# Attention scores, sums and weighted values on small float32 tiles of the array, in a cross-attention and expert block

## The reference

```
x   = x + xattn(layernorm(x), ctx)          # x (4, 512, 512), ctx (4, 64, 512)
x   = x + ffn(layernorm(x))

xattn: q = h Wq^T + bq, k = ctx Wk^T + bk, v = ctx Wv^T + bv      # 16 heads of 32
       p = softmax(where(attend, clip(q k^T / sqrt(32), +-50), -50))
       layernorm(rs * ((p v) Wo^T + bo)) * gamma + beta
ffn:   8 experts of width 16, the two with the largest router weights:
       sum_e gate_e * silu(h down_e^T) up_e^T
```

## Time and profile before

| | us |
|---|---|
| median of 2 runs | 241.1 (240.43 to 241.77) |
| profiled execution, its own time | 242.23 |
| its span | 240.5 |
| PE busy | 213.7 (89%) |
| DVE busy | 174.7 (73%) |
| ACT busy | 111.5 (46%) |
| POOL busy | 93.6 (39%) |

### The profile page before, as it was taken

The page is one execution under the profiler, slowest core; times in us unless marked ns, Lnnn a source line. Parts: engine busy times, 40 slices in busy tenths (PEclk is TensorE's granted clock), DMA queues, the critical chain, the costliest instruction groups (busy, mean ns, idle before and its releaser), DMA issues.

```text
span 240.5 us, 3478 instructions
## 1 busy us (share of the span) xinstructions
PE 213.7 (89%) x1184; PEld 170.8 (71%) x1184; DVE 174.7 (73%) x414; ACT 111.5 (46%) x196; POOL 93.6 (39%) x160
## 2 busy tenths in 40 slices
PE   0399999899999999999699999999999999997744
PEld 0288675488887778898486788987867898775622
DVE  2766295585769778839977888478968768989783
ACT  2454675366023579641345586525263732314720
POOL 5842002089964145201585326022673101326520
PEclk9999999999999999999999999999999999997985
DMA  7999300405000000000022000000211000001124
GB/s 221 286 393 307 149 3 0 145 33 177 0 0 0 3 0 0 4 0 0 0 90 87 0 3 0 0 4 0 87 47 41 3 0 3 0 1 44 44 104 157
DMA packets 9316, 14.65 MB, mean 61 GB/s; under 512 B 1618, under 2 KB 2642, under 8 KB 9300
## 3 DMA queue, kind: packets, MB, share of 16 engines
q1 hardware_dynamic: 8704, 14.44, 17.0%
q10 hardware_dynamic: 596, 0.01, 0.1%
HBM read 10.25 MB, written 4.19 MB: 60 GB/s over the span
## 4 chain that ended last, share of the span: by engine, by line
PE 70%; DVE 12%; ACT 7%; DMA 4%; issue 4%; POOL 1%; SPq 1%; DVEq 0%; ACTq 0%
PE ps_r L336 43%; PE ps_v L415 8%; PE ps_t L360 7%; PE ps_v L446 5%; PE ps_r L403 5%; DMA wk<-wk_t 4%; ACT wk L633 2%; DVE d_st L940 1%; ACT stage L650 1%; PE ps_v L449 1%; DVE ln_st L851 1%; DVE hs L946 1%; DVE stage L905 1%; ACT kbd L681 1%; ACT q_hi L638 1%
## 5 line engine op out<-in xcount | busy, mean ns | idle before, releaser
L415 PE MATMUL ps_v<-vbd,stage 128*128 128x66 f32 x256 | 31.5, 273 | 0.7 <-DVE stage L905 0.4
L415 PEld LDWEIGHTS ps_v<-vbd,stage 128*128 128x128 f32 x256 | 30.4, 192 | 1.7 <-issue 1.3
L614 ACT CAST attt_hi<-ps_t 128x512 fp32r<-128x512 f32 x32 | 17.8, 588 | 24.1 <-PE ps_t L360 23.7
L336 PE MATMUL ps_r<-hst_hi,wq_hi 128*128 128x512 f32 x64 | 26.3, 410 | 0.0
L638 ACT ACTIVATE q_hi<-ps_r,bq_sb 128x512 fp32r<-128x512 f32 x16 | 11.0, 689 | 31.3 <-PE ps_r L336 31.3
L336 PE MATMUL ps_r<-hst_hi,wq_lo 128*128 128x512 f32 x64 | 25.3, 395 | 0.0
L336 PE MATMUL ps_r<-wo_lo,attt_hi 128*128 128x512 f32 x64 | 25.3, 395 | 0.0
L336 PE MATMUL ps_r<-wo_hi,attt_hi 128*128 128x512 f32 x64 | 25.2, 394 | 0.0
L336 PE MATMUL ps_r<-wo_hi,attt_lo 128*128 128x512 f32 x64 | 25.2, 394 | 0.0
L336 PE MATMUL ps_r<-hst_lo,wq_hi 128*128 128x512 f32 x64 | 25.2, 394 | 0.0
L861 DVE TENSOR_TENSOR attt_lo<-ps_t,attt_hi 128x512 fp32r<-128x512 f32 x32 | 21.2, 684 | 3.9 <-ACT attt_hi L614 3.7
(11 more groups left out here) (115 smaller groups left out, 471.3 us busy)
## 6 DMA issues: line engine op xcount, KB each, us to landing
out<-xs SPq DMA_DIRECT2D x16, 256.0 KB, 2.0
xs<-x SPq DMA_DIRECT2D x3, 1024.0 KB, 5.5
xs<-x SPq DMA_DIRECT2D x2, 512.0 KB, 4.4
wk<-wk_t SPq DMA_DIRECT2D x1, 1024.0 KB, 9.7
stage<-wq_t SPq DMA_DIRECT2D x1, 1024.0 KB, 11.8
xs<-wv_t SPq DMA_DIRECT2D x1, 1024.0 KB, 13.9
xs<-wo_t SPq DMA_DIRECT2D x1, 1024.0 KB, 15.9
stage<-ctx_t SPq DMA_DIRECT2D x1, 512.0 KB, 6.1
```

The costliest lines, as they stand in the source:

```text
L336: last = pe.matmul(dst, w, m, start=start and i == 0, stop=stop and i == n - 1)
L415: mmi = pe.matmul(ps_v[k][:, i * VW:(i + 1) * VW], probs[:, p, t * P:(t + 1) * P], vbd[:, b, p, :], start=True, stop=True)
L614: act.copy(dst, ps_t[ring_t.bank(part, use)][:, 0:c * P].rearrange("p (c n) -> p c n", c=c)).then_inc(done, 1)
```

## The change

Scores: `scores(b, r)` now does half of the heads at a time, 8 plain float32 matmuls of 32 array rows by 64 columns, each with one head's keys as the stationary operand and its 512 query columns streamed; four row groups and two column halves make eight tiles. Query and key are no longer split, so `q_lo`, `k_hl` and `kbd` go, and ACT alone empties the query banks. Sums: `sums(b, g)` multiplies the exponentials by a matrix of ones and zeros, 16 matmuls of 128 rows by 32 columns with 128 streamed columns, four accumulated in each of four column groups; the reciprocals come out with 128 elements in a partition, and `spread` copies them by 16 `stream_shuffle` of 128 columns to all channels of a head. Weighted values: `weigh(b, g)` holds 64 by 32 values as the stationary operand and streams the 512 exponentials of a head, 8 matmuls to a group. The result is channels by tokens, so `att_transpose` goes, and `att` is split chunk by chunk; `project` waits for all four chunks. `x1t` gets a buffer of its own, `att` moves from `wk` to `hs`. All orders are written anew, with a first step of its own.

```diff
-R_STEP = ["S0", "S1", "S2", "S3", "q2", "q3", "S4", "S5", "S6", "S7", "Q0", "W0", "W1", "Q1", "U0", "U1", "U2", "U3",
-          "W2", "W3"]
-R_FIRST = ["S0", "S1", "S2", "S3", "q2", "q3", "V0", "V1", "S4", "S5", "S6", "S7", "Q0", "W0", "W1", "Q1", "W2", "W3"]
+R_STEP = ["S0", "S1", "S2", "S3", "q2", "q3", "S4", "S5", "S6", "S7", "Q0", "Q1", "W0", "W1", "U0", "U1", "U2", "U3", "W2", "W3"]
+R_FIRST = ["S0", "S1", "S2", "S3", "q2", "q3", "S4", "S5", "S6", "S7", "V0", "V1", "Q0", "Q1", "W0", "W1", "W2", "W3"]
...
-T_STEP = ["n0", "n1", "h0", "h1", "h2", "h3", "n2", "n3", "c0", "c1", "a0", "c2", "c3", "a1"]
-T_LAST = ["n0", "n1", "n2", "n3", "c0", "c1", "a0", "c2", "c3", "a1", "n0+", "n1+", "n2+", "n3+", "a0+", "a1+"]
-V_LAST = ["f0", "v00", "f1", "v01", "v10", "v11", "v20", "f2", "f3", "v21", "v30", "v31", "f0+", "f1+", "f2+", "f3+"]
-V_STEP = ["f0", "f1", "v00", "v01", "v10", "v11", "v20", "v21", "f2", "f3", "v30", "v31"]
+T_FIRST = ["h0", "h1", "h2", "h3"]
+T_STEP = ["n0", "n1", "h0", "h1", "h2", "h3", "n2", "n3", "a0", "a1"]
+T_LAST = ["n0", "n1", "n2", "n3", "a0", "a1", "n0+", "n1+", "n2+", "n3+", "a0+", "a1+"]
+V_LAST = ["f0", "f1", "s0", "f2", "s1", "f3", "v0", "v1", "v2", "v3", "f0+", "f1+", "f2+", "f3+"]
+V_FIRST = ["s0", "s1", "v0", "v1", "v2", "v3"]
+V_STEP = ["f0", "f1", "s0", "s1", "v0", "v1", "v2", "v3", "f2", "f3"]
...
         hs = sb("hs", [P, KC, H])
-        cen = hs
...
-        kbd = sb("kbd", [P, 2 * KC, 2 * T], F32R)
...
-        vbd = sb("vbd", [P, B, NP, VW])
+        k_sb = sb("k_sb", [P, KC, B * T])
+        v_sb = sb("v_sb", [P, B, 2, P])
+        sum_ones = sb("sum_ones", [P, NT, 4, 2 * NT])
         up_out = sb("up_out", [P, NT, H])
-        q_hi, q_lo = split("q", [P, KC, S])
+        q_sb = sb("q_sb", [P, KC, S])
...
         attt_hi, attt_lo = split("attt", [P, NT, KC, P])
-        x1t_hi, x1t_lo = attt_hi, attt_lo
+        x1t_hi, x1t_lo = split("x1t", [P, NT, KC, P])
...
-            def scores(b, c):
-                uses = [f"S{2 * c + i}" for i in range(2)]
-                out = [ps_r[take(b, use)] for use in uses]
-                for which, (k_part, q_part) in enumerate(((c, q_hi), (c, q_lo), (KC + c, q_hi))):
-                    for i in range(2):
-                        r = slice(2 * HD * i, 2 * HD * (i + 1))
-                        mmi = pe.matmul(out[i][:, :], kbd[r, k_part, :], q_part[r, c, :],
-                                        start=which == 0, stop=which == 2)
-                        if which == 2:
+            def scores(b, r):
+                wanted = [(b - 1, "Q0"), (b - 1, "Q1")] if r == 0 else [(b, "q2"), (b, "q3")]
+                pe.wait_ge(q_ok, max(ring_r.count(part, use) for part, use in wanted))
+                out = [ps_r[take(b, f"S{4 * r + i}")] for i in range(4)]
+                for j in range(2):
+                    c = 2 * r + j
+                    for i in range(4):
+                        rows_in = slice(HD * i, HD * (i + 1))
+                        mmi = pe.matmul(out[i][j * T:(j + 1) * T, :], k_sb[rows_in, c, b * T:(b + 1) * T],
+                                        q_sb[rows_in, c, :], start=True, stop=True)
+                        if j == 1 and i % 2 == 1:
                             mmi.then_inc(s_full, 1)
-            def weigh(b, t, g):
-                k = take_one(ring_v, b, f"v{t}{g}", v_free)
-                if t == 0:
-                    pe.wait_ge(probs_ok, KC * b + 2 * g + 2)
+            def sums(b, g):
+                k = take_one(ring_v, b, f"s{g}", v_free)
+                pe.wait_ge(probs_ok, KC * b + 2 * g + 2)
+                for n in range(NT):
+                    for i in range(4):
+                        mmi = pe.matmul(ps_v[k][HD * i:HD * (i + 1), 0:P],
+                                        sum_ones[:, n, :, :].rearrange("p a m -> p (a m)"),
+                                        probs[:, 4 * g + i, n * P:(n + 1) * P], start=n == 0, stop=n == NT - 1)
+                mmi.then_inc(v_full, 1)
+            def weigh(b, g):
+                bank = [ps_v[take_one(ring_v, b, f"v{2 * g + j}", v_free)] for j in range(2)]
                 for i in range(4):
-                    p = 4 * g + i
-                    mmi = pe.matmul(ps_v[k][:, i * VW:(i + 1) * VW], probs[:, p, t * P:(t + 1) * P],
-                                    vbd[:, b, p, :], start=True, stop=True)
-                mmi.then_inc(v_full, 1)
-            def att_transpose(b, t):
-                pe.wait_ge(v_free, ring_v.count(b, f"v{t}1"))
-                transposes(b, f"c{t}", chunks(att, t))
+                    for j in range(2):
+                        rows_in = slice(T * j, T * (j + 1))
+                        mmi = pe.matmul(bank[j][HD * i:HD * (i + 1), :], v_sb[rows_in, b, g, HD * i:HD * (i + 1)],
+                                        probs[rows_in, 4 * g + i, :], start=True, stop=True)
+                        if i == 3:
+                            mmi.then_inc(v_full, 1)
             def project(b, t):
...
-                pe.wait_ge(t_free, ring_t.count(b, f"c{t}"))
+                pe.wait_ge(attt_lo_ok, KC * (b + 1))
                 k = take(b, f"W{t}")
                 pairs = [(ones_k[:, :], bo_hl[:, :])]
...
+            def step(b):
+                x1n_transpose(b, b - 1, 0)
+                scores(b, 0)
+                query(b, 2)
+                x1n_transpose(b, b - 1, 1)
+                query(b, 3)
+                down(b, (0,))
+                down(b, (1,))
+                scores(b, 1)
+                hs_transpose(b, b + 1, 0)
+                hs_transpose(b, b + 1, 1)
+                hs_transpose(b, b + 1, 2)
+                sums(b, 0)
+                hs_transpose(b, b + 1, 3)
+                x1n_transpose(b, b - 1, 2)
+                x1n_transpose(b, b - 1, 3)
+                query(b, 0)
+                sums(b, 1)
+                query(b, 1)
+                weigh(b, 0)
+                weigh(b, 1)
+                down(b, (2,))
+                down(b, (3,))
+                hid_transpose(b, b - 1, 0)
+                project(b, 0)
+                project(b, 1)
+                up(b, 0)
+                hid_transpose(b, b - 1, 1)
+                up(b, 1)
+                up(b, 2)
+                up(b, 3)
+                project(b, 2)
+                project(b, 3)
...
+            def att_hi(b, c):
+                act.wait_ge(v_free, ring_v.count(b, f"v{c}"))
+                act.copy(attt_hi[:, :, c, :], att[:, c, :].rearrange("p (t n) -> p t n", t=NT)).then_inc(attt_hi_ok, 1)
...
+            def att_lo(b, c):
+                dve.wait_ge(attt_hi_ok, KC * b + c + 1)
+                dve.tensor_tensor(attt_lo[:, :, c, :], att[:, c, :].rearrange("p (t n) -> p t n", t=NT),
+                                  attt_hi[:, :, c, :].bitcast(F32), ALU.subtract).then_inc(attt_lo_ok, 1)
...
-            def normalise(b, halves):
-                def values_of(half):
-                    return ps_v[ring_v.bank(b, f"v{half}")][:, 0:4 * VW].rearrange("p (n w) -> p n w", n=4)
-                def reciprocals(half):
-                    t, g = int(half[0]), int(half[1])
-                    dve.wait_ge(v_full, ring_v.count(b, f"v{half}"))
-                    dve.reciprocal(rz[:, t, g, :, :], values_of(half)[:, :, 2 * HD:VW]).then_inc(rz_ok, 1)
-                def product(half):
-                    t, g = int(half[0]), int(half[1])
-                    order = [u[1:] for u in V_STEP if u[0] == "v"]
-                    dve.wait_ge(rz_ok, 2 * NT * b + order.index(half) + 1)
-                    dve.tensor_tensor(att[:, t, 4 * 2 * HD * g:4 * 2 * HD * (g + 1)].rearrange(
-                                          "p (n s d) -> p n s d", n=4, s=2),
-                                      values_of(half)[:, :, 0:2 * HD].rearrange("p n (s d) -> p n s d", s=2),
-                                      rz[:, t, g, :, :].unsqueeze(3).broadcast_to([P, 4, 2, HD]), ALU.mult
-                                      ).then_inc(v_free, 1)
-                reciprocals(halves[0])
-                for half, following in zip(halves, halves[1:]):
-                    reciprocals(following)
-                    product(half)
-                product(halves[-1])
+            def reciprocals(b, g):
+                dve.wait_ge(v_full, ring_v.count(b, f"s{g}"))
+                dve.reciprocal(rz[:, g, :], ps_v[ring_v.bank(b, f"s{g}")][:, 0:P]).then_inc(v_free, 1)
+            def spread(b, g):
+                dve.wait_ge(v_free, ring_v.count(b, f"s{g}"))
+                if b < B - 1:
+                    dve.wait_ge(t_full, ring_t.count(b, f"h{2 * g + 1}"))
+                for j in range(2):
+                    for n in range(NT):
+                        dve.stream_shuffle(att[:, 2 * g + j, n * P:(n + 1) * P], rz[:, g, :], [NT * j + n] * 32
+                                           ).then_inc(spread_ok, 1)
+            def product(b, c):
+                dve.wait_ge(spread_ok, 2 * NT * (2 * b + c // 2) + NT * (c % 2 + 1))
```

(47 more changed lines are left out.)

562 lines of the change are left out of this document (247 added, 315 removed).

## The result

The changed kernel takes 269.5 us (267.57 and 271.50) against 241.1 before: ratio 1.118, 95% interval 1.081 to 1.155. It is slower. The profiled execution is one of 267.57 us with a span of 265.8 (before 240.5). The time of 269.5 lies inside the range, 229 to 277, and "slower" had the largest of the three chances. But the number, 243, is 26 us too low, and the rival that stood for "slower" is not what happened: that the time lies in the range is luck, since the forecast case itself ended at 252 and the upper part of the range came from that rival.

What follows compares the result with a forecast made beforehand. PE was taken to bound the middle of the kernel. First element -3.0 us, elements 1 and 2 together -0.8, last +5.5: +1.7 on 241.1 gives 242.8, rounded to 243; range for 8 in 10, 229 to 277.

Steps and rivals of the forecast that it cites:

- the forecast case: Whole kernel: tiles run side by side but PE is held up by waits; 234 to 252 us, chance 0.40.
- The price of the tiles: PE's score, sum and value groups: all tiles of a group run at once, 1.1 us per group.
- The sum of -22.4 us: PE's matmul and transpose work over all four elements: 6.6 us replaces 12.2, so -5.6 per element.
- The slower rival: Small-tile groups: a float32 matmul's second record holds up the next tile in program order; 283 us, or 265; chance 0.30.
- scores behind the centring: An element's first scores need banks freed by centring the previous element's W3; +1.4 us, 1.9 in the last element.
- second weighing: In elements 1 and 2 it needs both banks of the first, so waits for two products and two hops; +1.6 us.
- down 2: In elements 1 and 2 it needs the bank of product 2, which stands behind att_lo 0 and 1; +1.1 us.
- Elements 1 and 2, transposes: Six groups share two banks; each third waits for a `_lo` subtraction behind clips on DVE: +0.2 and about +1.3 us.
- project 0's 0.6: In elements 1 and 2 it needs all four att_lo, the last behind a cross addition waiting for down 2; +0.6 us.
- The old wait of 2.2: PE's wait for DVE in the middle of the kernel before; expected to go, -2.2 us in each of elements 1 and 2.
- 3.1 us of old waits: First element: 1.1 for the value blocks and 2.0 from last scores to first weighing were to go, -3.1 us.
- the faster rival: Whole kernel: the new waits overlap instead of adding, half of about 30 us gone; 230 us, chance 0.27.

Runs made afterwards that it cites:

- e1_warm: Changed kernel plus 93 filler matmuls on constant operands placed where PE waited; 257.2 us, ratio 1.065.
- e4_split: Changed kernel with each score and value matmul cut into two of 256 columns, one behind the other on the same tile; 270.0 us, ratio 1.118.
- e10_beta: Changed kernel with POOL's beta additions of the first two elements moved away from the first element's att_lo, and value_blocks(1) moved; 269.2 us, ratio 1.114.
- e5_warm_less: Changed kernel with e1_warm's fillers, copies in place of the reciprocals and one shuffle per chunk instead of four; 257.4 us, ratio 1.065.
- e9_halves: Changed kernel with weighted values cut by tokens instead of heads, and some calls moved to suit; 260.1 us, ratio 1.075.
- e12_both_warm: e11_both plus 84 filler matmuls in ten places; 256.7 us, ratio 1.057.
- e8_scores_only: Kernel before with only its scores changed, to four small-tile float32 matmuls per chunk; 241.9 us, ratio 0.9985.
- e11_both: Changed kernel with the edits of e9_halves and e10_beta together; 258.3 us, ratio 1.064.
- e6_reorder: Changed kernel with the same instructions in another order, both queries ahead of the scores in elements 1 to 3; 285.5 us, ratio 1.176.

## Why the prediction was right or wrong

**The price of the tiles: right.** 1.1 us was forecast per group, 1.02 to 1.13 measured, 1.08 for the sums. The sum of -22.4 us can be read too: the end of PE's last matmul less its idle time is 237.35 - 14.65 = 222.7 us before; with the clock held (e1_warm), fillers left out, it is 252.38 - 51.63 = 200.8, a difference of 21.9, with 8 and 10 us of half clock in the two up to there.

**The slower rival: its mechanism is refuted** (e4_split), though the time lies in its 265 to 283. The Trainium skill ("TensorE: Matmul & The Clock Gate", Part 3) has matmuls in strict program order of start and end. The groups of the changed kernel fit this, with eight first records and then eight second ones. The first group of e4_split does not: eight records start 13 to 18 ns apart, and three more rounds of eight begin 0.24, 0.45 and 0.67 us behind the first. The records do not name their tile, but with eight to a round a tile's second matmul starts behind the first ones of tiles that come later in the program. Here the measurement decides, and neither the second record nor a second matmul of one tile holds back the next tile, which was my reading.

**The waits: most of the named ones were right, their sum was 11 us too small.** Single waits, forecast and measured: scores behind the centring 1.4 in elements 1 and 2 and 1.9 in the last, measured 1.8, 1.6 and 2.0; query 2 behind the exponential 1.2 and 1.2; second weighing 1.6 and 1.6; down 2 1.1 and 0.9. By windows, which put the wait for the centring in the element before, idle time was to rise by 4.0, 5.2, 5.7 and 9.2 us and rose by 10.3, 6.7, 9.1 and 9.4. What failed:
- Elements 1 and 2, transposes: 1.5 us was forecast for each element; 3.0 and 3.5 were measured, of which the first, 1.9 each time, was entered as 0.2, as if it replaced a wait of the first weighing; the trace of before has only 0.2 us of waiting by weighings in each of these elements.
- Elements 1 and 2, up 0: its wait for the copy of a query, 1.1 in each, was not in the sum. Against it, project 0's 0.6 did not come.
- The old wait of 2.2 was taken off twice, as if element 2 had one like it. Rows 1 shows 50.80 less 49.53, 1.3 us of idle time in all there.
- In the first element 3.1 us of old waits were taken off, but PE had been idle for 1.3 in it: the 2.0 between the last scores and the piece at 49.09 in the chain was PE's own transposes and the beginning of the weighing:
```profile
46.70 0.43 PE L403 MATMUL ps_r<-q_hi,kbd 64*128 64x512 f32 x2
47.06 1.09 PE L360 MATMUL ps_t<-ident,hs 128*128 128x128 f32 x8
47.99 2.21 PE L415 MATMUL ps_v<-vbd,stage 128*128 128x66 f32 x16
```
- Project 0 of the first element waited 5.3, not 3.6, which e10_beta puts down to POOL running beside att_lo. And the wait of query 0 there, 1.4, behind hs_lo, with value_blocks(1) ahead of it on VectorE, was not in the sum.
- In the last element the sum came out, but in part by luck. Up to the second weighing 4.2 us was forecast and 4.7 measured, of which 3.2 are for a gating that the prediction had put behind it, since hidden transposes stand between the two weighings; up to project 0 5.7 was forecast and 3.2 measured. Small waits that were not in the forecast fill the difference.

**The clock: named, not priced.** The last sentence of the prediction set it aside. It is nearly half of what is missing, 12 us by e1_warm. The half clock rose from 11 us, all in the tail, to 44, and the longer stretches come in or behind waits: at 64.9 (in the wait of 5.3), 116.1, 170.8, and from 215.1 through the three waits of the last element. The profile had a row for it: in the tail of before, where PE is busy for 14.89 of 25.00 us, the clock is 0.78. A forecast that adds 24 us of waits to elements which had 6 should have charged some of that, though no row could say how much: the wait of 2.2 us in element 1 of before left the clock at 1.00.

**The sum again.** From before to after, -22 of work, +36 of idle time (51.0 less 14.7) and +11 of half clock (after's 262.7 - 51.0 = 211.7, less e1_warm's 200.8) make +25, which is the difference of the two spans, 265.8 less 240.5. The forecast was -22.4 and +24.1. (In the faster rival, half of about 30 us is 15, and 13 was taken off; its chance of 0.27 did not hang on that.)

**The sizes of VectorE's operations: one wrong, harmless.** Reciprocal 0.94 for 0.29; shuffle and product right. e5_warm_less shows that they cost next to nothing on the path.

## What to carry to other kernels

A faster matmul form is worth its gain only where the engine stays fed: before counting the gain, list which piece of the output the next stage needs first, and whether the new layout gives it first. Here the layout by channels gave every token tile at once and late, and cutting by tokens, with the order changed to suit, took back a third of the loss (e9_halves) for the same matmul work. Where a change adds waits of 1 to 5 us to a stretch that had none, charge the clock too, from a stretch of the same trace that has such waits. Fillers show what the clock costs, but one that stands where PE does not wait is a cost itself (e12_both_warm). And subtract an old wait only once, from a stretch in which the idle time shows that it is there.

## What the runs showed of the hardware

- At full clock eight float32 matmuls of 512 columns on eight tiles take 1.02 to 1.13 us, four on four tiles 1.02 (e8_scores_only), and twice as many of 256 columns 1.18 (e4_split).
- A subtraction of 512 columns that reads two SBUF tensors took 0.92, 1.15 and 1.75 us beside POOL's additions of beta and 0.69 without them (e10_beta). The product, with one operand in PSUM, stayed at 0.68 to 0.69 in all 16. The Trainium skill ("GPSIMD Engine Reference", section 1, Specifications) says the same: POOL's SBUF interface contends with VectorE's instructions that have two SBUF inputs. The trace agrees, 798 ns against 687 in the mean. Before, att_lo read PSUM and an SBUF tensor, and four of them that ran beside additions of beta for their whole length took 0.68 to 0.69 as well; that the change moves it to two SBUF operands was in the diff.
- A reciprocal from PSUM takes 0.94 us for 128 columns and 0.19 for 8, so some 6 ns a column; an addition or a subtraction takes 0.29 for 136 and 0.69 for 512, some 1 ns a column (estimates from these rows).
- The granted clock is not the same in two executions of one order. The first half-clock stretch came at 32 us in e10_beta and e12_both_warm, at 39 to 42 in e1_warm, e9_halves and e11_both, at 65 in after and e6_reorder, and not before 237.6 in e5_warm_less; up to 50 us PE's program is the same in all of them. The two executions of after, 267.6 and 271.5 us, have mean granted clocks of 0.917 and 0.904, which is 44 and 52 us of half clock.
